# Two gathers of expert results that add into the residual during the transfer, and eight output stores in place of thirty-two

## What is computed

```
x = x + 0.5 * ffn(layernorm(x))
x = x + attention(layernorm(x))
x = x + 0.5 * ffn(layernorm(x))

def ffn(x):                       # 8 experts, one chosen per token
    logits = x @ gate_w.T
    sel, rw = argmax(logits), sigmoid(max(logits))
    for e in range(8):
        xs = x * (rw * (sel == e))[:, None]
        out += (xs @ w_up[e].T) * silu(xs @ w_gate[e].T) @ w_down[e].T
```

## Time and profile before

| what | value |
| --- | --- |
| time, median of 3 runs (lowest to highest) | 1230.92 us (1229.14 to 1231.17) |
| the profiled execution's own time | 1230.1 us |
| its span | 1228.3 us |
| PE busy | 1016.4 us (83% of the span) |
| DVE busy | 792.7 us (65%) |
| POOL busy | 676.9 us (55%) |
| ACT busy | 488.4 us (40%) |
| granted clock of PE, mean | 0.92 |

### The profile page before, as it was taken

The page is one execution under the profiler, slowest core; times in us unless marked ns, Lnnn a source line. Parts: engine busy times, 40 slices in busy tenths (PEclk is TensorE's granted clock), DMA queues, the critical chain, the costliest instruction groups (busy, mean ns, idle before and its releaser), DMA issues.

```text
span 1228.3 us, 17831 instructions
## 1 busy us (share of the span) xinstructions
PE 1016.4 (83%) x5480; PEld 586.1 (48%) x5481; DVE 792.7 (65%) x1211; ACT 488.4 (40%) x760; POOL 676.9 (55%) x385
## 2 busy tenths in 40 slices
PE   5839975499999989999998999998999999559800
PEld 4828842244444554444454444445455555538600
DVE  6565457657878746787873777877667744565431
ACT  1354431244444344444434444442445554344300
POOL 0025344277777627677644777773687785035371
PEclk9999956599999989999998999999999999669955
DMA  8055522000000100000010000001001000145453
GB/s 287 7 168 156 148 71 88 24 2 1 1 1 1 44 2 1 1 1 1 1 44 2 1 1 1 1 1 43 1 1 76 30 1 1 34 154 161 133 151 121
DMA packets 39484, 60.26 MB, mean 49 GB/s; under 512 B 5872, under 2 KB 33008, under 8 KB 38384
## 3 DMA queue, kind: packets, MB, share of 16 engines
q1 hardware_dynamic: 19424, 25.30, 5.8%
q0 software_dynamic: 6912, 18.88, 5.8%
q10 hardware_dynamic: 13072, 15.09, 3.5%
HBM read 30.81 MB, written 23.07 MB: 44 GB/s over the span
## 4 chain that ended last, share of the span: by engine, by line
PE 60%; DVE 11%; issue 9%; ACT 8%; POOL 7%; DMA 3%; ACTq 0%; DVEq 0%; POOLq 0%; SPq 0%
PE ps_o L928 14%; PE ps L913 9%; PE ps L560 6%; PE ps L720 5%; ACT arena_b L1120 5%; POOL arena_b L1322 5%; PE ps_x L700 4%; DVE maxes L726 3%; PE ps L916 3%; PE ps L1061 3%; PE ps L197 2%; PE ps_x L949 2%; ACT rows_store L476 2%; POOL arena_b L675 2%; PE ps L544 1%
## 5 line engine op out<-in xcount | busy, mean ns | idle before, releaser
L1322 POOL TENSOR_TENSOR arena_b<-arena_b 128x1024 f32<-128x1024 f32 x224 | 537.1, 2398 | 275.4 <-PE ps_o L928 168.7
L726 DVE TENSOR_REDUCE maxes<-ps 128x2 f32<-128x1024 f32 x256 | 311.7, 1218 | 184.0 <-PE ps L720 181.0
L1120 ACT ACTIVATE arena_b<-ps 128x1024 f32<-128x1024 f32 x256 | 255.8, 1024 | 190.7 <-PE ps L916 178.3
L928 PE MATMUL ps_o<-arena_b,latent_now 128*64 128x512 f32 x1024 | 261.6, 618 | 14.2 <-ACT arena_b L1120 5.3
L913 PE MATMUL ps<-q_split,keys_now 64*128 64x512 f32 x1536 | 223.5, 396 | 0.0
L509 POOL DMA_INDIRECT arena_b<-scaled_x,token_of x80 | 75.8, 947 | 178.5 <-issue 83.1
L913 PEld LDWEIGHTS ps<-q_split,keys_now 64*128 64x128 f32 x1536 | 147.1, 188 | 30.3 <-issue 2.4
L928 PEld LDWEIGHTS ps_o<-arena_b,latent_now 128*64 128x64 f32 x1024 | 53.1, 135 | 150.2 <-ACT arena_b L1120 132.9
L1239 DVE RECIPROCAL rows_store<-rows_store 128x256 f32<-128x256 f32 (+1 forms) x72 | 112.6, 1565 | 12.0 <-ACT rows_store L1131 12.0
L916 PE MATMUL ps<-q_shift 64*128 64x512 f32 x512 | 101.9, 393 | 0.0
L675 POOL DMA_INDIRECT arena_b<-sorted_y,slots x64 | 60.8, 950 | 67.2 <-DVE x_res L683 27.9
(11 more groups left out here) (175 smaller groups left out, 1127.1 us busy)
## 6 DMA issues: line engine op xcount, KB each, us to landing
sorted_y<-arena_b ACTq DMA_DIRECT2D x80, 128.0 KB
scaled_x<-rows_store SPq DMA_DIRECT2D x32, 256.0 KB, 2.1
x_res<-x_in SPq DMA_DIRECT2D x4, 1024.0 KB, 13.0
keys_now<-keys_next SPq DMA_DIRECT2D x4, 1024.0 KB, 4.6
out<-x_res SPq DMA_DIRECT2D x32, 128.0 KB
arena_a<-w_gu SPq DMA_DIRECT2D x1, 2048.0 KB, 16.0
arena_a<-w_gu ACTq DMA_DIRECT2D x1, 2048.0 KB, 7.7
arena_b<-scaled_x,token_of POOLq DMA_INDIRECT x80
```

The lines of the kernel that those rows point to most:

```text
L726: nc.vector.tensor_reduce(maxes[:, 2 * m:2 * m + 2], ps[2][:, :, :], AX_X, ALU.max) \
L928: last = nc.tensor.matmul(ps_o[h, :], latent_now[:, kt, :], src, start=(kt == 0), stop=(kt == KT - 1))
L1120: nc.scalar.activation(dst, ps_s[n % 2][:, :, :], ACT.Exp, scale=SCALE).then_inc(sem("exp_done"), 1)
L1322: nc.gpsimd.tensor_tensor(t, t, probs[kt % PROBS].rearrange("p a n -> p (a n)"), ALU.add) \
```

## The change

Three things change. ACT's `y_out` multiplies by 0.5, so `sorted_y` holds halved results. The indirect transfer adds them onto `x_tile(t)` itself, with `compute_op=ALU.add`; the buffers, DVE's addition and POOL's wait for it are gone. Its semaphores count groups of four tiles instead of buffers, so whoever waits for a tile waits for its group. The loop of 32 output stores becomes eight written-out stores of four tiles (512 KB), each behind its group's semaphore.

```diff
-                nc.scalar.activation(y_rows[:, k, :], banks[6 + k % 2][:, 0:D], ACT.Copy) \
+                nc.scalar.activation(y_rows[:, k, :], banks[6 + k % 2][:, 0:D], ACT.Copy, scale=0.5) \
                     .then_inc(sem(f"y_ready_{tag}"), 1)
...
             for t in range(NT):
                 k = t % RING
-                if t >= RING:
-                    pool.wait_ge(sem(f"ffn_added_{tag}"), t - RING + 1)
...
-                pool.indirect_dma_start(rows_back[:, k, :], None, sorted_y[:, :],
-                                        bass.IndirectOffsetOnAxis(ap=slots[:, t:t + 1], axis=0)) \
-                    .then_inc(sem(f"gathered{k}_{tag}"), 16)
+                pool.indirect_dma_start(x_tile(t), None, sorted_y[:, :],
+                                        bass.IndirectOffsetOnAxis(ap=slots[:, t:t + 1], axis=0),
+                                        compute_op=ALU.add).then_inc(sem(f"gathered{t // RING}_{tag}"), 16)
 
         def dve_gathered(dve, tag, i, k):
 
             t = RING * i + k
-            dve.wait_ge(sem(f"gathered{k}_{tag}"), 16 * i + 16)
-            nc.vector.scalar_tensor_tensor(x_tile(t), rows_back[:, k, :], 0.5, x_tile(t),
-                                           ALU.mult, ALU.add).then_inc(sem(f"ffn_added_{tag}"), 1)
-            if tag == "f1":
-                dve.wait_ge(sem(f"ffn_added_{tag}"), t + 1)
-                tile_stats(t, "att")
-
-        def dve_gather(dve):
-            with dve.Fori(0, NT // RING) as i:
-                for k in range(RING):
-                    dve_gathered(dve, "f2", i, k)
-            dve.wait_ge(sem("ffn_added_f2"), NT)
+            dve.wait_ge(sem(f"gathered{i}_{tag}"), 16 * RING)
+            tile_stats(t, "att")
...
-            with sp.Fori(0, NT) as t:
-                col = sp.snap(t * D)
-                sp.wait_ge(sem("ffn_added_f2"), t + 1)
-                sp.dma_start(out_tiles[:, ds(t, 1), :], x_res[:, ds(col, D)].unsqueeze(1)) \
+            for g in range(NT // RING):
+                sp.wait_ge(sem(f"gathered{g}_f2"), 16 * RING)
+                sp.dma_start(out_tiles[:, g * RING:(g + 1) * RING, :],
+                             x_res[:, g * RING * D:(g + 1) * RING * D].rearrange("p (t d) -> p t d", d=D)) \
                     .then_inc(sem("out_stored"), 16)
-            sp.wait_ge(sem("out_stored"), 16 * NT)
+            sp.wait_ge(sem("out_stored"), 16 * NT // RING)
...
-                else:
-                    dve_gather(dve)
```

## The result

| what | before | after |
| --- | --- | --- |
| time, median (lowest to highest) | 1230.92 us (1229.14 to 1233.3, 5 runs) | 1237.36 us (1235.85 to 1237.82, 5 runs) |
| ratio to before, 95% interval | | 1.0053 (1.0038 to 1.0068) |
| the profiled execution's own time | 1230.1 us | 1236.15 us |
| its span | 1228.3 us | 1234.3 us |

I had predicted 1211.0 us. The page after has this: the span; POOL's queue by packets, MB and share of the 16 DMA engines; the gathers; the stores.

The account below looks back on a forecast made before the run. SP's loop of 32 output stores was taken to bound the end. Opening -2.3, end -17.8 and later landing +1.0 gave -19.1 us, so 1211.0 us against the profiled 1230.1; whole range 1207 to 1254, likeliest case 1207 to 1216.

Parts of the forecast that it names:

- Rival C: End: SP stays slow during gathers, leaving three stores for afterwards; about +4, 1215 us; counted inside the 0.48 forecast case.
- The adding transfer's pace: POOL's gathers in both stretches: instruction stays 0.95 us, gathers stay 1.25 us apart, so no change.
- its own threshold, 0.48 us: Extra time per gather, over 40 gathers, from which the predicted 19.1 us gain is gone; a pace of 1.73 us.
- rival A: POOL's gather instruction doubles to 1.90 us and its pace binds: 1251 us; full A or B beyond 1.73 us pace: 0.33.
- The end: From the last gather's landing to the span's end: new end 1210.5 against 1228.3 us, -17.8 us.
- after the last 128 KB store the span ran 0.4 us further: End: 0.4 us from the last store's landing to the span's end, carried over to the new end.
- The store's 2.9 us: End: the last 512 KB store takes 2.9 us, placed between 256 KB in 2.1 us and 1024 KB in 4.6.
- The adding transfer's landing: Both stretches: adding gathers land 0.5 us later in each, +1.0 us in all.
- rival B: DMA engines bind at 3 to 5 times 0.46 us per gather: 1217 to 1253; beyond 1.73 us, with full A: 0.33.
- The opening: Start of the attention: 0.92 - 0.84 - 0.88 - 0.67 - 0.82 = -2.3 us, before +0.5 for later landing.
- the 0.84 us of the row pairs: Opening, four row pairs: without DVE's sums PE binds at about 1.15 us a pair; 3 x 0.28 = -0.84.
- 0.88 + 0.67 + 0.82: Opening, DVE sums removed: two query-split rounds -0.88, the shift's round -0.67, two sums behind the 16th maximum -0.82.

Follow-up runs that it names:

- add_f1: stores8 with the adding transfer in the first feed-forward block only; 1218.86 us, 5.15 above stores8 on the same chip.
- stores8: Kernel before, additions still on DVE, with only the eight written-out output stores; 1213.71 us, ratio 0.9966; repeated on another chip (stores8_b) 1215.6 us, 0.9871.
- before_again: The kernel before, unchanged, run again for its trace; 1232.86 us, ratio 1.0003 to the same kernel's comparison runs.
- drain4: stores8 with four more plain gathers behind the last one, into space nothing reads; 1221.94 us, 4.9 above stores8 on its chip.
- mix12: add_f1 with the adding transfer only from tile 12 on; 1216.2 us, ratio 0.9868, and on another chip 1214.52 us, 0.9871.
- add_f2: stores8 with the adding transfer in the second feed-forward block only; 1234.66 us, ratio 1.0029, beside stores8 at 1217.03 us.
- add_stores32: The changed kernel with 32 written-out stores of one tile, each behind its group's semaphore; 1237.99 us, ratio 1.0174.
- forms: stores8 with 32 more gathers behind the last, four each of eight plain or adding forms, into free space; 1277.38 us with the added work.
- loop8: Kernel before with output stores of four tiles each in a loop of eight turns with register work; 1213.87 us, ratio 0.9855.
- stores32: Kernel before with its 32 one-tile output stores written out, without the loop; 1216.03 us, ratio 0.9996, and on another chip 1217.78 us, 0.9893.

## Why the prediction was wrong

**What bound the end: right.** SP's loop did, and the written-out stores took it out of the way. Rival C did not happen: each of the eight stores is 0.37 or 0.38 us and on time.

**The adding transfer's pace: the step that failed.** "I take no change of the pace: the DMA engines, two thirds idle, are not what sets it, and the gap of 0.30 us ... shows that part of POOL's turn is not descriptors at all." The first half held and says nothing about POOL's own instruction; the second is about the 0.30 us, which stayed, not about the 0.95, which rose by 0.60. So POOL's instruction, put at no change, became the bound in both stretches. The text had its own threshold, 0.48 us, its own sign of being wrong, an instruction above 1.4 us, and rival A, with its price, on the far side. It gave 1251 us for a full doubling. With the measured 0.60 its formula gives -19.1 + 40 x 0.60 = +4.9, and the profiled execution showed +6.05. That they lie so close is partly luck: the formula has no DRAIN (2.2 us too little at the end, below), and the first gather's 0.8 us are no effect of the change. A was right in where the loss would come and wrong in why: it took the 0.95 us for a count of rows, and the extra 0.59 are mostly a fixed cost.

**The end: 20.6 us mis-sized, in two terms.** Predicted from the first gather to the end were 1210.5 - 1165.1 + 0.5 = 45.9 us; it is 66.5. Of this the pace has 18.0 (57.22 - 39.21) and the longer last instruction 0.6. The other term is "after the last 128 KB store the span ran 0.4 us further": behind the landed stores it ran 2.6 us (1231.7 to 1234.3), since POOL's DRAIN ends last. Had the pace stayed, the DRAIN alone would have put the end at about 1214 instead of 1210.5. The store's 2.9 us are as predicted (1228.80 to 1231.7).

**The adding transfer's landing and the DMA engines: right.** It lands about 0.3 to 0.5 us later behind its instruction (predicted 0.5). POOL's queue from 1167 to 1229 us, the window that holds the second block's 32 gathers:

```profile
q0 software_dynamic: 4608, 4.20, 49.2%
```

That is 0.492 x 62 us / 32 gathers = 0.95 us each, against the 0.93 that the prediction made of two reads; rival B is out. The queue's packets are 144 a gather, 4608/32, and were 48 (576/12). The Trainium skill (Collectives: The Full Stack, The bandwidth ceiling) has an adding transfer, in its collectives, at half the rate of a copy; on the DMA engines this agrees (0.95 us against 0.46), but they don't set the time. The Trainium skill (DMA: Bandwidth & Descriptors, Anatomy of one DMA) also says that many descriptors can be written before their number begins to cost, and the 0.9 and 2.0 ns a row agree. What I had drawn from it, that the pace stays, doesn't follow: the cost isn't in their number.

**The opening: wrong up to the latents for the pace, right behind them.** Predicted was -2.3 + 0.5 = -1.8 us, measured is +2.1. Up to PE's first latent product it went wrong: that begins 184.77 - 155.71 = 29.06 us behind the first gather and was 23.42, so +5.6 where the terms gave +0.6. The first three groups come 0.60 us a gather later, and DVE waits for each; the 0.84 us of the row pairs can't come in, since DVE waits 2.33 us for the third group between them. Behind it 3.6 us came back, where 0.88 + 0.67 + 0.82 = 2.4 were predicted. In rows of PE, the first and the last product of the maxima, and where the clock falls, after and then before:

```profile
199.74 0.51 PE L708 MATMUL ps<-keys_next,q_split 64*128 64x512 f32 x2
...
205.21 0.50 PE L708 MATMUL ps<-keys_next,q_split 64*128 64x512 f32 x2 [1.32 <-DVE maxes L714]
...
207.04 0.80 PE L708 MATMUL ps<-keys_next,q_split 64*128 64x512 f32 x2 [1.32 <-DVE maxes L714]
...
230.39 0.80 PE L708 MATMUL ps<-keys_next,q_split 64*128 64x512 f32 x2 [1.32 <-DVE maxes L714]
```

```profile
193.55 0.50 PE L720 MATMUL ps<-keys_next,q_split 64*128 64x512 f32 x2
195.38 0.50 PE L720 MATMUL ps<-keys_next,q_split 64*128 64x512 f32 x2 [1.32 <-DVE maxes L726]
197.29 0.80 PE L720 MATMUL ps<-keys_next,q_split 64*128 64x512 f32 x2 [1.42 <-DVE maxes L726]
...
226.60 0.79 PE L720 MATMUL ps<-keys_next,q_split 64*128 64x512 f32 x2 [1.32 <-DVE maxes L726]
```

From the first product to the last it is 30.65 us and was 33.05, so 2.4 less. A product of 0.50 us is one at the full clock, one of 0.80 at half of it: the granted clock reads 1.00 from 199.8 to 205.6 us and 0.50 from 207.1 to 230, that is 2.4 and 1.2 GHz. After the change four rounds run at the full clock instead of two, each 1.83 us instead of 2.12: 0.6. The other 1.8 answer to the predicted 0.88 + 0.67. From the last product to PE's row behind the maxima it is 8.55 us and was 9.47, 0.92 less (predicted 0.82), and up to the first product 0.2 less. So each of these terms was about right. The clock's share is this execution's: the changed kernel run as an experiment, and `add_f1`, had two rounds at the full clock as before, and their 16 maxima take 31.2 us. Up to PE's row the four traces with adding gathers in the whole opening have 82.2 to 85.2 us, the eleven with the opening of before 78.9 to 82.8. Their means, 83.2 and 80.4, are 2.8 us apart: the loss is there, but one pair of traces doesn't size it.

The 2.1 us are also too few, because the kernel before is late by itself in both of its traces. ACT stands still 2.23 us before the last copy that precedes the root of the statistics, and DVE then waits for that root. Before, and under it ACT's row in `stores8_b`:

```profile
168.26 0.38 ACT L1433 ACTIVATE w_vo<-ps 64x256 f32<-64x256 f32 x1 [2.23 <-PE ps L1462]
...
170.20 0.20 DVE L309 RECIPROCAL st<-st 128x8 f32<-128x8 f32 x1 [1.42 <-issue]
```

```profile
166.34 0.38 ACT L1433 ACTIVATE w_vo<-ps 64x256 f32<-64x256 f32 x1 [0.76 <-issue]
```

PE's first transposes begin 17.4 us behind the first gather, in `before_again` 18.3, and in the nine other traces with the same opening code 16.1 to 16.3; in those ACT stands still 0.8 to 1.0 us there and DVE 0.3. What delays ACT is open. The latents begin 22.1 to 22.7 us behind the first gather in the nine and 29.1 to 29.4 in the four with adding gathers. These 7 us, less 1.8 in the maxima and 0.9 behind them, leave an estimate of 4.3 for what the transfer costs in the opening at an equal clock, nearer to the 5.15 us of `add_f1` than 2.1 is. By the same rows some 1 to 2 us of what `stores8` gains on the kernel before lie in the opening and not in SP's loop.

## What to carry to other kernels

Handing arithmetic to an indirect transfer moves its price to the engine that issues it; where that engine sets the pace, as POOL does here, 0.60 us of issue per transfer weighs more than the 0.42 us of an addition that lay beside it on another engine. When you remove what ends last, look up every engine's closing instructions for the next to end, since a DRAIN may be long and covered. On a queue's engine write few large stores out rather than loop over many small ones, when they run beside gathers: here the loop of 32 fell behind on the traced chips, and 32 written-out stores cost 2.2 us more than eight. A loop of eight did no worse than eight written out.

## What the runs showed of the hardware that was not expected

- An indirect transfer that adds takes POOL 1.54 us with 128 rows and 1.35 with 32; a plain one 0.95 and 0.86. The bytes of a row (256 or 1024) change nothing.
- POOL's closing DRAIN ends 8.8 to 9.1 us behind the last gather's instruction where both blocks gather plainly (before, `stores8` on three chips, `drain4`), 8.2 to 8.4 where only gathers of the first block add (`add_f1`, `mix12`), 7.5 to 7.6 where those of the second do (after, `add_f2`, `add_stores32`), and 10.5 in `forms`, though the rows land about 2 us behind the instruction. What it waits for is not shown.
- In three traces (before, `before_again`, `loop8`) SP's loop takes up to 8.4 us a turn beside gathers, with single queue instructions of 0.7 and 1.2 us instead of 0.34 to 0.39, and before 0.89 us once they are over. Written-out stores on the same chip are not slowed. The kernel before takes 1217 us on one chip and 1230 to 1232 on three others, and the cause of that stays open.
- 32 small stores beside the gathers lengthen single gather instructions from 0.95 to as much as 1.17 us (`stores32`); beside eight large ones all read 0.95 (`stores8`). Why is not shown.
